# Negative maxima sent to the score rows in two parts, and one matmul fill for q, k and v with the rotary halves crossed by VectorE

## The chip, the cores and the metric

The kernel runs on one core of one Trainium2 chip. The metric is the device time of one execution in microseconds, the median over runs. Beside it there is one profiled execution, whose trace gives the span and the start and length of the instructions. Engines are named as the profile names them: PE (TensorE matmuls; PEld its weight loads), DVE (VectorE), ACT (ScalarE), POOL (GpSimd), SP (SyncE, which issues all DMAs here).

## The reference

One pre-norm decoder layer on 16 batches of 100 tokens by 128 features, in float32: causal self-attention with a rotary embedding, cross-attention with 16 heads of 64 over 1444 context rows of 96 features, and a ternary linear layer on quantized activations. Each adds to its input.

```python
def _apply_rope(t, cos, sin):
    te = t[..., 0::2]
    to = t[..., 1::2]
    oe = te * cos + to * sin
    oo = -te * sin + to * cos
...
x = x + _L0_attn_ref(_layernorm(x), wq, wk, wv)            # softmax(rope(q) rope(k)^T / sqrt(128)) v
x = x + _L0_xattn_ref(_layernorm(x), ctx_768, Wq, Wk, Wv, Wo, bo)
x = x + _L0_ffn_ref(_layernorm(x), ternary_weight, bias, act_scale)
```

## The kernel before

**Batches and steps.** Work goes batch by batch (16), a batch b in `STEPS` = 24 steps. In the cross-attention the 16 x 100 queries form Q = 1600 columns, cut in `NB` = 4 blocks of 400 (`BLK`); the 1444 keys, padded, form 12 chunks of 128. A step takes two chunks against one block, so a block is 6 steps (`BSTEPS`). In each step PE does three groups of scores (L1086: high times high, and two cross terms with the low parts) and three groups of values for the step two earlier (L1116). ACT takes the exponential twice (L615, L617), DVE makes the low part of the probabilities (`pr_lo`, L887, or L881 and L883 in a block's first step, where L881 works on partitions 64 to 99).

**Fills.** Everything else that PE does is a "fill": a small matmul into one of three PSUM banks, put between the six groups of a step by the hand-written table `AT`, and emptied ("consumed") by DVE in the same order. A fill may start when the fill three before it has been consumed (`misc_free`). A tuple in `AT` is (what, number, how many batches ahead). `MAXES` says how many of the 39 "max" fills stand in each step: they compute the scores of batch b+1 in high precision only, 13 query tiles of 128 by 3 pieces of 482 keys, and DVE reduces each (L666) to a row maximum, which the softmax needs.

**Negative maxima.** After the 39th piece DVE reduces `maxes` to `negmax` [128, 13]; the fill "negmax" in step 21 transposes it (L954); DVE copies it to `negmaxT` [13, 128] (L687); and SP sends it with two DMAs (L398, L400) into the last partition of `q_hi` of batch b+1, where the first score matmul adds it through a row of ones. PE waits for it (`row_in_s`) at the first score of a batch. Batch 0 is different: its first 7 tiles (`FIRST`, which cover 896 of 1600 queries, the first two blocks) get their maxima before the batch starts ("negmax_a"), the other 6 inside its first 9 steps ("max_b", "negmax_b").

**Self-attention.** It runs two batches ahead, one fill per stage: T1 (transposed input), QK, V, S, PT, AO, T2, in steps 3, 4, 5, 6, 8, 12 and 15. The host stacks five weights: q, q with its halves swapped, k, k with its halves swapped, v. QK makes four matmuls (L960) so that DVE can multiply q and k by cosines (L694) and the swapped ones by sines (L696) and add them (L701), all on 128 partitions. V is one matmul (L963), copied by L703.

**Loop.** Batch 0 is written out, batches 1 to 12 are a loop of 6 rounds of two batches on every engine, batches 13 to 15 are written out. The loop jumps back five times: at the starts of batches 3, 5, 7, 9 and 11. `START` lists what runs before batch 0: T1, QK, V and S of batches 0 and 1 in turn, with the four products M = Wq Wk^T by head (L1011) between them, then the first q blocks (L931) and the first maxima (L1049).

Of the kernel before, what the change touches and what calls it, by code (L numbers as in the profile page):

```python
# [35 lines left out]
def decoder_layer(nc, x_in, ctx_in, ctx_last_in, ctxT_in, wself_in, wqT_in, wkT_in, wvT_in, wo_in, bo_in,  # L36
# [4 lines left out]
    B, S, D = x_in.shape  # L41
# [34 lines left out]
    with ExitStack() as stack:  # L76
# [19 lines left out]
        wself = sb("wself", [D, 5, D])  # L96
# [28 lines left out]
        negmaxT = sb("negmaxT", [QT, P], F32R)  # L125
# [91 lines left out]
        SELF = ("T1", "QK", "V", "S", "PT", "AO", "T2")  # L217
        START = [("T1", 0), ("T1", 1), ("QK", 0), ("V", 0), ("QK", 1), ("V", 1), ("S", 0), ("S", 1),
# [5 lines left out]
        INPUT = {"QK": ("T1",), "V": ("T1",), "AO": ("PT",), "q": ("T2",), "F": ("T3",)}  # L224
# [7 lines left out]
        for what, s in zip(SELF[:-1], (3, 4, 5, 6, 8, 12)):  # L232
            AT[s].append((what, 0, 2))
# [6 lines left out]
        AT[MAX_END].append(("negmax", 0, 1))  # L240
# [15 lines left out]
        BATCH_0 = ("max_b", "negmax_b")  # L256
        for k in range(FIRST * PIECES, QT * PIECES):
            AT[(k - FIRST * PIECES) // 2].append(("max_b", k, 0))
# [40 lines left out]
        def use_of(b, wanted):  # L299

            return next(use for step in body_uses(b) for what, _, _, use, _ in step if what == wanted)
# [59 lines left out]
        def _(sp):  # L361
# [31 lines left out]
            def move_negmax(n, par, use, first=0):  # L393


                sp.wait_ge(misc_free, use + 1)
                full = Q // P
                sp.dma_start(q_hi[par][DC:DC + 1, first * P:full * P].bitcast(F32),  # L398
                             negmaxT[0:full - first, :].bitcast(F32)).then_inc(row_in_s, 16)
                sp.dma_start(q_hi[par][DC:DC + 1, full * P:Q].bitcast(F32),  # L400
                             negmaxT[full - first:QT - first, P - (Q - full * P):P].bitcast(F32)).then_inc(row_in_s, 16)
# [8 lines left out]
            def store(n, par, use):  # L410
# [5 lines left out]
            sp.wait_ge(misc_free, NSTART)  # L416
            sp.dma_start(q_hi[0][DC:DC + 1, 0:FIRST * P].bitcast(F32),
                         negmaxT[0:FIRST, :].bitcast(F32)).then_inc(row_a_in_s, 16)

            def body(b, par):  # L420
                ahead = b + 2 if isinstance(b, int) else sp.snap(b + 2)
                before = b - 1 if isinstance(b, int) else sp.snap(b - 1)
                if present(b, 0, "negmax_b"):
                    move_negmax(0, 0, use_of(0, "negmax_b"), FIRST)
                if present(b, -1):
                    move_sums(b - 1, 1 - par)
                if present(b, 2):
                    split_done(b + 1)
                    load_ctx(ahead)
                if present(b, -1):  # L430
                    store(before, 1 - par, use_of(b, "F"))
                if present(b, 1):
                    move_negmax(b + 1, 1 - par, use_of(b, "negmax"))
# [201 lines left out]
        def _(dve):  # L635
            order = Order(dve, vchain, 10)
# [18 lines left out]
            def consume(n, par, what, j, use, bank):  # L655
# [8 lines left out]
                elif what == "max":  # L664
                    t, p = divmod(j, PIECES)
                    nc.vector.tensor_reduce(maxes[:, t, p:p + 1], here[:, 0:PW], AX.X,  # L666
                                            ALU.max).then_inc(misc_free, 1)
                    if j == QT * PIECES - 1:
                        dve.wait_ge(misc_free, use + 1)
                        nc.vector.tensor_reduce(negmax[:, :], maxes[:, :, :], AX.X, ALU.max,  # L670
                                                negate=True).then_inc(negmax_done, 1)
# [8 lines left out]
                elif what == "negmax_a":  # L680
                    nc.vector.tensor_copy(negmaxT[0:FIRST, :], here[0:FIRST, 0:P]).then_inc(misc_free, 1)
                elif what == "negmax_b":
                    dve.wait_ge(row_a_in_s, 16)
                    nc.vector.tensor_copy(negmaxT[0:QT - FIRST, :], here[0:QT - FIRST, 0:P]).then_inc(misc_free, 1)
                elif what == "negmax":
                    at_least(dve, row_in_s, n * 32)
                    nc.vector.tensor_copy(negmaxT[:, :], here[0:QT, 0:P]).then_inc(misc_free, 1)  # L687
# [118 lines left out]
            for what, n in START[2:8]:  # L806
                start(what, n)
# [3 lines left out]
            for what, n in START[8:10]:  # L811
                start(what, n)
# [106 lines left out]
        def _(pe):  # L919
            def fill(n, par, what, j, use, bank, behind, ring=FILLS):  # L920
# [25 lines left out]
                elif what == "negmax_a":  # L946
                    pe.wait_ge(negmax_a_done, 1)
                    mm = nc.tensor.transpose(here[0:FIRST, 0:P], negmax[:, 0:FIRST], ident[:, :])
                elif what == "negmax_b":
                    pe.wait_ge(negmax_done, 1)  # L950
                    mm = nc.tensor.transpose(here[0:QT - FIRST, 0:P], negmax[:, FIRST:QT], ident[:, :])
                elif what == "negmax":
                    pe.wait_ge(negmax_done, n + 1)
                    mm = nc.tensor.transpose(here[0:QT, 0:P], negmax[:, :], ident[:, :])  # L954
# [3 lines left out]
                elif what == "QK":  # L958
                    for m in range(4):
                        mm = nc.tensor.matmul(here[:, m * S:(m + 1) * S], wself[:, m, :], xnT[par][:, :],  # L960
                                              start=True, stop=True)
# [67 lines left out]
            for what, n in START[2:6]:  # L1029
# [34 lines left out]
            def scores(b, par, s, i):  # L1064
# [135 lines left out]
```

## Time and profile before

| what | value |
|---|---|
| median of 3 runs | 1172.28 us (1171.85 to 1172.44) |
| the profiled execution's own time | 1173.88 us |
| its span | 1170.9 us |
| PE busy | 1136.2 us, 97% |
| DVE busy | 934.5 us, 80% |
| ACT busy | 695.5 us, 59% |
| POOL busy | 232.1 us, 20% |
| DMA | 24.40 MB, mean 21 GB/s |

The first row is what a change is measured by; the second and third belong to the execution that was traced. A busy share is an average over the span. What the time hangs on is told by the chain of work that ended last, and by what PE waited for.

### The profile page before, as it was taken

The numbers are of one execution on the slowest core, as the hardware profiler recorded it, in microseconds if no ns is written. First come the engines' busy times: TensorE is split into PE (matmuls) and PEld (weight loads), VectorE is DVE, ScalarE is ACT, GpSimd is POOL, SyncE is SP. The second block draws the span as 40 slices with busy tenths as digits, with TensorE's granted clock in tenths as the row PEclk, the third lists the DMA queues.
The fourth block names the chain that finished last, engine by engine and source line by source line (L and its number), as shares of the span: only waits on it lengthen the run. The fifth ranks groups of instructions, "written<-read, shape, count | busy, mean of one in ns | idle before, by whom it ended". The sixth has DMA issues, their size and how long they took to land.

```text
span 1170.9 us, 20390 instructions
## 1 busy us (share of the span) xinstructions
PE 1136.2 (97%) x6561; PEld 1047.5 (89%) x6561; DVE 934.5 (80%) x1691; ACT 695.5 (59%) x1001; POOL 232.1 (20%) x228
## 2 busy tenths in 40 slices
PE   6799999999999999999999999999999999999996
PEld 5588999998999899998999989999899999999995
DVE  3698888887888788787978878898788888878645
ACT  1155656656575665756657565665656566575653
POOL 3120130312203022130302213030221303112010
PEclk9799999999999999999999999999999999999998
DMA  7101010010101001010010101001010100100000
GB/s 151 41 1 42 2 41 4 1 42 5 41 3 41 4 2 40 4 41 5 9 36 1 41 5 41 3 2 42 3 41 3 41 3 2 42 2 1 3 1 4
DMA packets 12727, 24.40 MB, mean 21 GB/s; under 512 B 4934, under 2 KB 8654, under 8 KB 12494
## 3 DMA queue, kind: packets, MB, share of 16 engines
q1 hardware_dynamic: 12622, 23.00, 7.4%
q8 instruction: 65, 1.06, 0.4%
q14 instruction: 40, 0.33, 0.1%
HBM read 21.88 MB, written 0.82 MB: 19 GB/s over the span
## 4 chain that ended last, share of the span: by engine, by line
PE 91%; DVE 5%; issue 3%; ACT 1%; DMA 1%; POOL 0%; DVEq 0%; SPq 0%; POOLq 0%; ACTq 0%
PE banks L1086 35%; PE banks L1116 31%; PE banks L940 10%; PE banks L978 4%; PE banks L931 4%; PE banks L960 1%; DVE pr_lo L887 1%; PE banks L1021 1%; DVE maxes L666 1%; PE banks L1011 1%; PE banks L1049 0%; DMA q_hi<-negmaxT 0%; DVE maxes L674 0%; DVE xn L650 0%; ACT banks L617 0%
## 5 line engine op out<-in xcount | busy, mean ns | idle before, releaser
L615 ACT ACTIVATE pr_hi<-banks 128x800 fp32r<-128x800 f32 x384 | 322.4, 840 | 393.4 <-PE banks L1086 393.4
L666 DVE TENSOR_REDUCE maxes<-banks 128x1 f32<-128x482 f32 x585 | 370.4, 653 | 57.6 <-PE banks L940 53.8
L887 DVE TENSOR_TENSOR pr_lo<-banks,pr_hi 128x800 fp32r<-128x800 f32 x320 | 315.0, 985 | 56.8 <-ACT banks L617 56.4
L617 ACT ACTIVATE banks<-banks 128x800 f32<-128x800 f32 x384 | 319.8, 833 | 0.0
L940 PE MATMUL banks<-cT_hi,q_hi 96*128 96x482 f32 x585 | 223.6, 382 | 1.4 <-DVE maxes L666 1.4
L1086 PE MATMUL banks<-q_hi,cT_hi 97*128 97x400 f32 x768 | 216.7, 363 | 8.3 <-DMA q_hi<-negmaxT 7.4
L1116 PE MATMUL banks<-pr_hi,cN_hi 128*97 128x400 f32 x768 | 214.2, 346 | 0.1
L1086 PE MATMUL banks<-q_hi,cT_lo 96*128 96x400 f32 x768 | 208.5, 352 | 0.0
L1086 PE MATMUL banks<-q_lo,cT_hi 96*128 96x400 f32 x768 | 204.4, 347 | 0.0
L1116 PE MATMUL banks<-pr_hi,cN_lo 128*96 128x400 f32 x704 | 190.6, 344 | 0.0
L1116 PE MATMUL banks<-pr_lo,cN_hi 128*97 128x400 f32 x704 | 190.6, 344 | 0.0
L1086 PEld LDWEIGHTS banks<-q_hi,cT_hi 97*128 97x128 f32 x768 | 134.0, 191 | 22.1 <-issue 9.5
L1086 PEld LDWEIGHTS banks<-q_lo,cT_hi 96*128 96x128 f32 x768 | 143.4, 190 | 0.0
L1086 PEld LDWEIGHTS banks<-q_hi,cT_lo 96*128 96x128 f32 x768 | 138.6, 189 | 3.8
L1116 PEld LDWEIGHTS banks<-pr_hi,cN_hi 128*97 128x97 f32 x768 | 124.0, 163 | 12.9 <-ACT o_sb L580 0.4
L1116 PEld LDWEIGHTS banks<-pr_hi,cN_lo 128*96 128x96 f32 x704 | 113.9, 162 | 17.1
L1116 PEld LDWEIGHTS banks<-pr_lo,cN_hi 128*97 128x97 f32 x704 | 114.2, 162 | 16.1
L482 POOL TENSOR_TENSOR ve<-mv,eps 100x1 f32<-100x1 f32 x48 | 9.2, 192 | 568.7 <-DVE mv L645 568.7
L940 PEld LDWEIGHTS banks<-cT_hi,q_hi 96*128 96x128 f32 x585 | 110.0, 188 | 9.2 <-DVE maxes L666 2.2
L513 POOL TENSOR_TENSOR o_sb<-o_sb,rball 96x1600 f32<-96x1600 f32 x15 | 54.6, 3642 | 106.1 <-issue 92.3
L931 PEld LDWEIGHTS banks<-x2T,M 128*96 128x96 f32 x512 | 56.6, 172 | 4.6 <-ACT G L585 1.0
L931 PE MATMUL banks<-x2T,M 128*96 128x100 f32 x512 | 58.0, 259 | 1.1 <-ACT G L585 0.7
(116 smaller groups left out, 887.6 us busy)
## 6 DMA issues: line engine op xcount, KB each, us to landing
cT_raw<-in_ctxT SPq DMA_DIRECT2D x16, 568.5 KB
cN_raw<-in_ctx SPq DMA_DIRECT2D x16, 528.0 KB
out<-result SPq DMA_DIRECT2D x16, 50.0 KB
X<-in_x SPq DMA_DIRECT2D x1, 700.0 KB
cN_raw<-in_ctx_last SPq DMA_DIRECT2D x16, 40.5 KB
wqT<-in_wqT SPq DMA_DIRECT2D x1, 512.0 KB, 5.4
wo<-in_wo SPq DMA_DIRECT2D x1, 512.0 KB, 13.2
wkT<-in_wkT SPq DMA_DIRECT2D x1, 384.0 KB, 7.2
```

Of the source, the lines that this page charges most:

```text
L513: nc.gpsimd.tensor_tensor(out=o_sb[par][0:DC, :], in0=o_sb[par][0:DC, :], in1=rball[:, :], op=ALU.mult).then_inc(on_done, 1)
L615: nc.scalar.activation(pr_hi[:, s % RING, :].rearrange("p (a q) -> p a q", a=2), pair, ACT.Exp, scale=float(DH) ** -0.5).then_inc(hi_done, 1)
L617: nc.scalar.activation(pair, pair, ACT.Exp, scale=float(DH) ** -0.5).then_inc(exp_done, 1)
L666: nc.vector.tensor_reduce(maxes[:, t, p:p + 1], here[:, 0:PW], AX.X, ALU.max).then_inc(misc_free, 1)
L887: nc.vector.tensor_tensor(pr_lo[:, s % RING, :].rearrange("p (a q) -> p a q", a=2), banks[:, slot:slot + 2, 0:BLK], pr_hi[:, s % RING, :]. ...
L931: mm = nc.tensor.matmul(here[0:DC, i * S:(i + 1) * S], M[:, h, :], x2T[par][:, :], start=True, stop=True)
L940: mm = nc.tensor.matmul(here[:, 0:PW], q_hi[par][0:DC, qtile(t):qtile(t) + P], cT_hi[par][0:DC, PAT[p]:PAT[p] + PW], start=True, stop=True)
L960: mm = nc.tensor.matmul(here[:, m * S:(m + 1) * S], wself[:, m, :], xnT[par][:, :], start=True, stop=True)
L978: mm = nc.tensor.matmul(here[0:S, 0:D], o_sb[par][0:DC, h * S:(h + 1) * S], G[:, h, :], start=(h == 0), stop=(h == H - 1))
L1011: mm = nc.tensor.matmul(banks[:, j, i * DC:(i + 1) * DC], wqT[:, 4 * j + i, :], wkT[:, 4 * j + i, :], start=True, stop=True)
L1086: mm = nc.tensor.matmul(banks[:, ST + 2 * (s % 2) + a, 0:BLK], k, q[:, blk * BLK:(blk + 1) * BLK], start=(i == 0), stop=(i == 2))
L1116: mm = nc.tensor.matmul(banks[0:m, OUT, 0:BLK], k, e[:, r, cols], start=(first and a == 1 and i == 0), stop=(s % BSTEPS == BSTEPS - 1 and ...
```

## The change

Two edits. First, every batch now sends its negative maxima in two parts, as batch 0 did: the part of the first 7 tiles is reduced after the 21st piece (step 11), transposed by a fill in step 12 and sent by a DMA of its own; the other 6 tiles go as before in step 21. The two parts have their own tiles `negmaxT_a` and `negmaxT_b`. PE waits for part a at a batch's first score and for part b at the first step of its third block. Second, the fills QK and V become one fill QKV in step 4, without the swapped weights: DVE multiplies by the sines in two instructions of 64 partitions, each reading one half of the partitions and writing the other, then copies V, then adds.

```diff
-        wself = sb("wself", [D, 5, D])
+        wself = sb("wself", [D, 3, D])
-        negmaxT = sb("negmaxT", [QT, P], F32R)
+        negmaxT_a = sb("negmaxT_a", [FIRST, P], F32R)
+        negmaxT_b = sb("negmaxT_b", [QT - FIRST, P], F32R)
-        for what, s in zip(SELF[:-1], (3, 4, 5, 6, 8, 12)):
+        for what, s in zip(SELF[:-1], (3, 4, 6, 8, 12)):
-        AT[MAX_END].append(("negmax", 0, 1))
+        AT[12].append(("negmax_a", 0, 1))
+        AT[MAX_END].append(("negmax_b", 0, 1))
...
+            def move_negmax_a(n, par, use):
+
+                sp.wait_ge(misc_free, use + 1)
+                sp.dma_start(q_hi[par][DC:DC + 1, 0:FIRST * P].bitcast(F32),
+                             negmaxT_a[:, :].bitcast(F32)).then_inc(row_a_in_s, 16)
...
+                    if j == FIRST * PIECES - 1:
+                        dve.wait_ge(misc_free, use + 1)
+                        nc.vector.tensor_reduce(negmax[:, 0:FIRST], maxes[:, 0:FIRST, :], AX.X, ALU.max,
+                                                negate=True).then_inc(negmax_a_done, 1)
...
-                elif what == "QK":
-
-                    v = here[:, 0:4 * S].rearrange("p (a m s) -> p a m s", a=2, m=2)
+                elif what == "QKV":
+
+                    v = here[:, 0:2 * S].rearrange("p (a s) -> p a s", a=2)
                     at_least(dve, rope_done, n)
-                    order.mark(nc.vector.tensor_tensor(rt[:, :, :], v[:, :, 0, :],
-                                                       cosT[:, :].unsqueeze(1).to_broadcast([D, 2, S]), ALU.mult))
-                    nc.vector.tensor_tensor(rt2[:, :, :], v[:, :, 1, :],
-                                            sinT[:, :].unsqueeze(1).to_broadcast([D, 2, S]),
-                                            ALU.mult).then_inc(misc_free, 1)
-                    dve.wait_ge(misc_free, use + 1)
+                    order.mark(nc.vector.tensor_tensor(rt[:, :, :], v, cosT[:, :].unsqueeze(1).to_broadcast([D, 2, S]),
+                                                       ALU.mult))
+                    for to, of in ((slice(0, D // 2), slice(D // 2, D)), (slice(D // 2, D), slice(0, D // 2))):
+                        turned = nc.vector.tensor_tensor(rt2[to, :, :], v[of, :, :],
+                                                         sinT[of, :].unsqueeze(1).to_broadcast([D // 2, 2, S]), ALU.mult)
+                    order.mark(turned)
+                    nc.vector.tensor_copy(V[par][:, :], here[0:S, 2 * S:2 * S + D]).then_inc(misc_free, 1)
                     order.wait()
                     nc.vector.tensor_tensor(qk[par][:, :, :], rt[:, :, :], rt2[:, :, :], ALU.add).then_inc(rope_done, 1)
-                elif what == "V":
-                    nc.vector.tensor_copy(V[par][:, :], here[0:S, 0:D]).then_inc(misc_free, 1)
...
-                elif what == "QK":
-                    for m in range(4):
...
-                elif what == "V":
-                    mm = nc.tensor.matmul(here[0:S, 0:D], xnT[par][:, :], wself[:, 4, :], start=True, stop=True)
+                elif what == "QKV":
+                    for m in range(2):
+                        nc.tensor.matmul(here[:, m * S:(m + 1) * S], wself[:, m, :], xnT[par][:, :], start=True, stop=True)
+                    mm = nc.tensor.matmul(here[0:S, 2 * S:2 * S + D], xnT[par][:, :], wself[:, 2, :],
+                                          start=True, stop=True)
...
-                    if isinstance(b, int) and b == 0:
-                        pe.wait_ge(row_a_in_s, 16)
-                    else:
-                        pe.wait_ge(row_in_s, (b + 1) * 32)
+                    pe.wait_ge(row_a_in_s, (b + 1) * 16)
                     pe.wait_ge(cTlo_done, b + 1)
-                if blk == 2 and s % BSTEPS == 0 and i == 0 and isinstance(b, int) and b == 0:
-                    pe.wait_ge(row_in_s, 32)
+                if blk == 2 and s % BSTEPS == 0 and i == 0:
+                    pe.wait_ge(row_in_s, (b + 1) * 32)
```

In the instruction order (operation, output<-inputs, shape, times repeated; names as in the code) this is PE in steps 4 and 5 of the loop's first batch, before:

```order
L960 MATMUL banks<-xnT,wself 128x100 x4
L1116 MATMUL banks<-pr_hi,cN_hi 97x400 x2
L1116 MATMUL banks<-pr_hi,cN_lo 96x400 x2
L1116 MATMUL banks<-pr_lo,cN_hi 97x400 x2
L212 REGISTER_ALU
L940 MATMUL banks<-cT_hi,q_hi 128x482
L212 REGISTER_ALU
L1086 MATMUL banks<-q_hi,cT_hi 128x400 x2
L1086 MATMUL banks<-q_lo,cT_hi 128x400 x2
L212 REGISTER_ALU
L963 MATMUL banks<-wself,xnT 100x128
```

And the same place of the changed kernel:

```order
L967 MATMUL banks<-xnT,wself 128x100 x2
L968 MATMUL banks<-wself,xnT 100x128
L1119 MATMUL banks<-pr_hi,cN_hi 97x400 x2
L1119 MATMUL banks<-pr_hi,cN_lo 96x400 x2
L1119 MATMUL banks<-pr_lo,cN_hi 97x400 x2
L213 REGISTER_ALU
L950 MATMUL banks<-cT_hi,q_hi 128x482
L213 REGISTER_ALU
L1089 MATMUL banks<-q_hi,cT_hi 128x400 x2
L1089 MATMUL banks<-q_lo,cT_hi 128x400 x2
```

Two of the four q and k matmuls are gone, and the V matmul has moved from step 5 to stand behind the other two. DVE at the same place, before:

```order
L694 TENSOR_TENSOR rt<-banks,cosT 128x200
L696 TENSOR_TENSOR rt<-banks,sinT 128x200
L353 REGISTER_ALU
L701 TENSOR_TENSOR qk<-rt 128x200
L657 REGISTER_ALU
L666 TENSOR_REDUCE maxes<-banks 128x1
L875 REGISTER_ALU
L887 TENSOR_TENSOR pr_lo<-banks,pr_hi 128x800
L657 REGISTER_ALU
L703 COPY V<-banks 100x128
```

And changed:

```order
L705 TENSOR_TENSOR rt<-banks,cosT 128x200
L708 TENSOR_TENSOR rt<-banks,sinT 64x200 x2
L711 COPY V<-banks 100x128
L357 REGISTER_ALU
L713 TENSOR_TENSOR qk<-rt 128x200
L666 REGISTER_ALU
L675 TENSOR_REDUCE maxes<-banks 128x1
L885 REGISTER_ALU
L897 TENSOR_TENSOR pr_lo<-banks,pr_hi 128x800
```

One multiply became two, and the copy of V now stands ahead of the addition and of step 4's `pr_lo`. PE in step 12 of the same batch, changed; before, the same rows stood there without the one that reads `negmax`, and with the max fill (there L940) behind the first value group:

```order
L977 MATMUL banks<-V,prT 100x128
L1089 MATMUL banks<-q_hi,cT_lo 128x400 x2
L213 REGISTER_ALU
L950 MATMUL banks<-cT_hi,q_hi 128x482
L1119 MATMUL banks<-pr_hi,cN_hi 97x400 x2
L1119 MATMUL banks<-pr_hi,cN_lo 96x400 x2
L213 REGISTER_ALU
L958 MATMUL banks<-ident,negmax 7x128
L1119 MATMUL banks<-pr_lo,cN_hi 97x400 x2
```

One transposing matmul has been added between the value groups. The number of fills of a batch stays what it was: V is gone, negmax_a has come.

## Rows read from the trace of the kernel before

**Rows 1.** The page's busy times: us, share of span, instructions.
```profile
PE 1136.2 (97%) x6561; PEld 1047.5 (89%) x6561; DVE 934.5 (80%) x1691; ACT 695.5 (59%) x1001; POOL 232.1 (20%) x228
```

**Rows 2.** What PE waited for between 60 and 1130 us: us, times, longest.
```profile
PE banks L1086 <- DMA q_hi<-negmaxT: 4.9, 5, 1.1
PE banks L940 <- DVE maxes L666: 1.4, 2, 1.2
```

**Rows 3.** Timeline, batch starts 2 and 3: start, us, engine, line [idle before <-releaser].
```profile
195.30 0.28 DVE L687 CAST negmaxT<-banks 13x128 fp32r<-13x128 f32 x1 [0.57 <-PE banks L954]
199.38 0.53 PE L1086 MATMUL banks<-q_hi,cT_hi 97*128 97x400 f32 x2
...
269.07 0.62 PE L1086 MATMUL banks<-q_hi,cT_hi 97*128 97x400 f32 x2 [1.05 <-DMA q_hi<-negmaxT]
271.67 1.01 DVE L773 CAST cT_hi<-cT_raw 96x758 fp32r<-96x758 f32 x2 [2.12 <-issue]
```

**Rows 4.** Chain that ended last, at batch 0's start and batch 11's: start, us, what.
```profile
56.55 0.25 issue
...
817.35 0.12 PE banks L954
818.77 3.31 DMA q_hi<-negmaxT
822.08 0.68 issue
```

**Rows 5.** The same chain in steps 4 and 5 of batch 4.
```profile
349.90 0.87 PE banks L960 x8
352.82 0.22 PE banks L963 x2
```

**Rows 6.** The same chain before batch 0.
```profile
7.82 2.01 PE banks L960 x8
10.62 2.03 PE banks L960 x8
13.07 1.95 PE banks L1011 x8
```

**Rows 7.** SP's timeline, and the page's DMA issues: KB each, us from issue to landing.
```profile
3.65 0.59 SPq L367 DMA_DIRECT2D wkT<-in_wkT  x1
...
wkT<-in_wkT SPq DMA_DIRECT2D x1, 384.0 KB, 7.2
```

**Rows 8.** Stretches: length, busy us of PE, PEld, DVE, ACT, POOL, PEclk, DMA, GB/s.
```profile
62.00:63.00 1.00, 1.00 (x4) 0.93 (x4) 0.99 (x3) 0.00 (x0) 0.24 (x2) 0.50 0.00 0
63.00:64.00 1.00, 1.00 (x6) 0.72 (x5) 0.91 (x2) 0.48 (x1) 1.00 (x2) 0.96 0.00 0
70.00:80.00 10.00, 10.00 (x66) 9.20 (x67) 9.79 (x18) 5.16 (x10) 0.00 (x0) 1.00 0.01 2
```

**Rows 9.** DVE's timeline in batch 0, steps 4 to 6.
```profile
73.19 0.37 DVE L694 TENSOR_TENSOR rt<-banks,cosT 128x200 f32<-128x200 f32 x1 [0.17 <-PE banks L960]
73.48 0.35 DVE L696 TENSOR_TENSOR rt<-banks,sinT 128x200 f32<-128x200 f32 x1
73.87 0.37 DVE L701 TENSOR_TENSOR qk<-rt 128x200 f32<-128x200 f32 x1
74.15 0.66 DVE L666 TENSOR_REDUCE maxes<-banks 128x1 f32<-128x482 f32 x1
...
82.25 1.22 DVE L674 TENSOR_REDUCE maxes<-banks 128x1 f32<-128x482 f32 x2
83.49 0.58 DVE L881 TENSOR_TENSOR pr_hi<-banks,pr_hi 36x400 fp32r<-36x400 f32 x1
84.08 0.57 DVE L883 TENSOR_TENSOR pr_lo<-banks,pr_hi 128x400 fp32r<-128x400 f32 x1
```

**Rows 10.** DVE and PE in steps 4 and 5 of batch 4.
```profile
350.81 0.37 DVE L694 TENSOR_TENSOR rt<-banks,cosT 128x200 f32<-128x200 f32 x1 [0.30 <-PE banks L960]
353.46 0.52 PE L1116 MATMUL banks<-pr_hi,cN_hi 128*97 128x400 f32 x2
```

More of the change, by code:

```diff
@@ L212, in at_least @@
                 eng.wait_ge(s, value)
-        SELF = ("T1", "QK", "V", "S", "PT", "AO", "T2")
-        START = [("T1", 0), ("T1", 1), ("QK", 0), ("V", 0), ("QK", 1), ("V", 1), ("S", 0), ("S", 1),
+        SELF = ("T1", "QKV", "S", "PT", "AO", "T2")
+        START = [("T1", 0), ("T1", 1), ("QKV", 0), ("QKV", 1), ("S", 0), ("S", 1),
                  ("PT", 0), ("PT", 1), ("AO", 0), ("T2", 0)] + [("q", j) for j in range(QB)] + [
@@ L221, in decoder_layer @@
         NSTART = len(START)
-        INPUT = {"QK": ("T1",), "V": ("T1",), "AO": ("PT",), "q": ("T2",), "F": ("T3",)}
+        INPUT = {"QKV": ("T1",), "AO": ("PT",), "q": ("T2",), "F": ("T3",)}
         GBANKS = [OUT, SIDE, MISC, MISC + 1]
@@ L256, in decoder_layer @@
         BATCH_0 = ("max_b", "negmax_b")
+        assert FIRST * P >= 2 * BLK and sum(MAXES[:12]) >= FIRST * PIECES
         for k in range(FIRST * PIECES, QT * PIECES):
@@ L297, in body_uses, with use_of @@
             return found
-        def use_of(b, wanted):
-            return next(use for step in body_uses(b) for what, _, _, use, _ in step if what == wanted)
+        def use_of(b, wanted, number=0, of=None):
+            return next(use for step in body_uses(b) for what, j, away, use, _ in step
+                        if (what, j) == (wanted, number) and of in (None, away))
         def batches(eng, body):
@@ L391, in split_done, with move_negmax_b @@
                 sp.wait_ge(last_done, n + 1)
-            def move_negmax(n, par, use, first=0):
+            def move_negmax_a(n, par, use):
+                sp.wait_ge(misc_free, use + 1)
+                sp.dma_start(q_hi[par][DC:DC + 1, 0:FIRST * P].bitcast(F32),
+                             negmaxT_a[:, :].bitcast(F32)).then_inc(row_a_in_s, 16)
+            def move_negmax_b(n, par, use):
                 sp.wait_ge(misc_free, use + 1)
                 full = Q // P
-                sp.dma_start(q_hi[par][DC:DC + 1, first * P:full * P].bitcast(F32),
-                             negmaxT[0:full - first, :].bitcast(F32)).then_inc(row_in_s, 16)
+                sp.dma_start(q_hi[par][DC:DC + 1, FIRST * P:full * P].bitcast(F32),
+                             negmaxT_b[0:full - FIRST, :].bitcast(F32)).then_inc(row_in_s, 16)
                 sp.dma_start(q_hi[par][DC:DC + 1, full * P:Q].bitcast(F32),
-                             negmaxT[full - first:QT - first, P - (Q - full * P):P].bitcast(F32)).then_inc(row_in_s, 16)
+                             negmaxT_b[full - FIRST:QT - FIRST, P - (Q - full * P):P].bitcast(F32)).then_inc(row_in_s, 16)
             def move_sums(n, par):
@@ L429, in body @@
                     load_ctx(ahead)
+                if present(b, 1):
+                    move_negmax_a(b + 1, 1 - par, use_of(b, "negmax_a"))
                 if present(b, -1):
@@ L635, in _ @@
         def _(dve):
-            order = Order(dve, vchain, 10)
+            order = Order(dve, vchain, 11)
             order.base = 0
@@ L667, in consume @@
                                             ALU.max).then_inc(misc_free, 1)
+                    if j == FIRST * PIECES - 1:
+                        dve.wait_ge(misc_free, use + 1)
+                        nc.vector.tensor_reduce(negmax[:, 0:FIRST], maxes[:, 0:FIRST, :], AX.X, ALU.max,
+                                                negate=True).then_inc(negmax_a_done, 1)
                     if j == QT * PIECES - 1:
                         dve.wait_ge(misc_free, use + 1)
-                        nc.vector.tensor_reduce(negmax[:, :], maxes[:, :, :], AX.X, ALU.max,
+                        nc.vector.tensor_reduce(negmax[:, FIRST:QT], maxes[:, FIRST:QT, :], AX.X, ALU.max,
                                                 negate=True).then_inc(negmax_done, 1)
@@ L680, in consume @@
                 elif what == "negmax_a":
-                    nc.vector.tensor_copy(negmaxT[0:FIRST, :], here[0:FIRST, 0:P]).then_inc(misc_free, 1)
+                    at_least(dve, row_a_in_s, n * 16)
+                    nc.vector.tensor_copy(negmaxT_a[:, :], here[0:FIRST, 0:P]).then_inc(misc_free, 1)
                 elif what == "negmax_b":
-                    dve.wait_ge(row_a_in_s, 16)
-                    nc.vector.tensor_copy(negmaxT[0:QT - FIRST, :], here[0:QT - FIRST, 0:P]).then_inc(misc_free, 1)
-                elif what == "negmax":
@@ L686, in consume @@
                     at_least(dve, row_in_s, n * 32)
-                    nc.vector.tensor_copy(negmaxT[:, :], here[0:QT, 0:P]).then_inc(misc_free, 1)
+                    nc.vector.tensor_copy(negmaxT_b[:, :], here[0:QT - FIRST, 0:P]).then_inc(misc_free, 1)
                 elif what == "T1":
                     nc.vector.tensor_copy(xnT[par][:, :], here[:, 0:S]).then_inc(misc_free, 1)
-                elif what == "QK":
-                    v = here[:, 0:4 * S].rearrange("p (a m s) -> p a m s", a=2, m=2)
+                elif what == "QKV":
+                    v = here[:, 0:2 * S].rearrange("p (a s) -> p a s", a=2)
@@ L805, in _ @@
             dve.wait_ge(self_in_s, 16 * 3)
-            for what, n in START[2:8]:
+            for what, n in START[2:6]:
                 start(what, n)
@@ L810, in _ @@
             high_T(0, 0, 1)
-            for what, n in START[8:10]:
+            for what, n in START[6:8]:
                 start(what, n)
@@ L946, in fill @@
                 elif what == "negmax_a":
-                    pe.wait_ge(negmax_a_done, 1)
+                    pe.wait_ge(negmax_a_done, n + 1)
                     mm = nc.tensor.transpose(here[0:FIRST, 0:P], negmax[:, 0:FIRST], ident[:, :])
                 elif what == "negmax_b":
-                    pe.wait_ge(negmax_done, 1)
+                    pe.wait_ge(negmax_done, n + 1)
                     mm = nc.tensor.transpose(here[0:QT - FIRST, 0:P], negmax[:, FIRST:QT], ident[:, :])
-                elif what == "negmax":
-                    pe.wait_ge(negmax_done, n + 1)
-                    mm = nc.tensor.transpose(here[0:QT, 0:P], negmax[:, :], ident[:, :])
                 elif what == "T1":
@@ L957, in fill @@
                     mm = nc.tensor.transpose(here[:, 0:S], xn1[par][:, :], ident[0:S, 0:S])
-                elif what == "QK":
-                    for m in range(4):
-                        mm = nc.tensor.matmul(here[:, m * S:(m + 1) * S], wself[:, m, :], xnT[par][:, :],
-                                              start=True, stop=True)
-                elif what == "V":
-                    mm = nc.tensor.matmul(here[0:S, 0:D], xnT[par][:, :], wself[:, 4, :], start=True, stop=True)
+                elif what == "QKV":
[3 more added lines that the diff above has]
+                                          start=True, stop=True)
                 elif what == "S":
@@ L1028, in _ @@
             pe.wait_ge(self_in_s, 16 * 3)
-            for what, n in START[2:6]:
+            for what, n in START[2:4]:
                 start(what, n)
@@ L1169 @@
     order = np.concatenate([np.arange(0, D, 2), np.arange(1, D, 2)])
-    swapped = np.concatenate([order[D // 2:], order[:D // 2]])
     wq, wk, wv = (np.asarray(w) for w in (L0_attn_wq, L0_attn_wk, L0_attn_wv))
-    wself = np.stack([wq[order].T, wq[swapped].T, wk[order].T, wk[swapped].T, wv.T], axis=1)
+    wself = np.stack([wq[order].T, wk[order].T, wv.T], axis=1)
     i = np.arange(D // 2, dtype=np.float32)
@@ L1187 @@
         "fbias": np.asarray(L0_ffn_bias), "ascale": np.asarray(L0_ffn_act_scale).reshape(1, 1),
-        "cos": np.concatenate([cos, cos]), "sin": np.concatenate([sin, -sin]), "last": last,
+        "cos": np.concatenate([cos, cos]), "sin": np.concatenate([-sin, sin]), "last": last,
     }
```

8 lines of the change are left out of this document (3 added, 5 removed).

## The prediction

> **What bounds the kernel now.** I read the page first. PE is busy 97% of the span, DVE 80% [rows 1], so a microsecond of PE work taken from the loop should be a microsecond of time, unless PE then waits. The waits say how often it does: from 60 to 1130 us PE waits 4.9 us in five pieces for the DMA of the negative maxima and 1.4 us in two pieces for a reduction by DVE, the next largest cause [rows 2]. So two things could be won: the 4.9 us of waiting, and PE work.
>
> The timeline shows where the five pieces are: PE stands idle 1.05 us before the first score at 269.07, the start of batch 3 [rows 3]. The other four lie at the starts of batches 5, 7, 9 and 11. These are the five places where the loop jumps back. Batch 2 starts at 199.38 with no idle time in its row, only 4.08 us after DVE began the copy of its maxima [rows 3]. The same copy and the same DMAs stand at the same place in every batch. At the jump DVE too stands idle, 2.12 us before its first instruction at 271.67, and the trace lays that on issue, on no data [rows 3]. So the label "DMA" on PE's idle time is suspect: a wait is there, but the engine would not have run without it. The chain says the same for batch 11: the DMA lands at 822.08 and PE starts 0.68 us later, where before batch 0, with no jump, it starts 0.25 us after the landing [rows 4]. The landing was not what ended the wait.
>
> **The first edit: maxima in two parts.** It takes the first score's wait for the late DMA away; part a is sent a half batch earlier. By the argument above the price of what it removes is 0, with the jump as what covers it. The other bound is 4.9 us [rows 2], if the label is right and the engine could start at once. I take 0. The rule of the Trainium skill, page "Runtime: NRT & Kernel Launch", section "Instruction fetch mechanics", is that a taken branch to code outside the small instruction buffer makes the engine wait for a fetch. By that rule the idle time stays at all five places and the sum stays as below; by the label it would be 4.9 us lower. The trace sides with the rule: the 2.12 us of DVE.
>
> What it adds: one transposing fill more in batches 0 to 14. L954 takes 0.12 us of the chain [rows 4]; its cost is in the 128 columns that pass, not in the 13 or 7 that are loaded, so each of the two parts costs that. In batches 1 to 14: 14 x 0.115 = +1.6 us. DVE gets one reduction and one copy more, about 0.3 us a batch, in steps 11 and 12. SP gets one DMA, behind the context loads, due only at the next batch, some 30 us later. The wait for part b moves to the third block, 12 steps after its DMA. All of that is hidden by PE's own work.
>
> **The second edit: QKV.** The fill QK, four matmuls in eight passes, takes 0.87 us of the chain in the loop [rows 5], 0.109 a pass. Four passes go: 0.435 us a batch. V's 0.22 [rows 5] only moves. The fills for batches 3 to 15 run in batches 1 to 13: 13 x 0.435 = -5.7 us.
>
> DVE pays. Now its instructions start 0.29, 0.39 and 0.28 us after one another: 73.19, 73.48, 73.87, 74.15 [rows 9], 0.96 in all. Afterwards there are two sine multiplies. Each still has 200 elements per partition, so I give each the 0.36 us of the full one; less is the lower bound. They also start at partition 64 or write there. What such a change does is seen at L881, on partitions 64 to 99: a reduction ends at 82.25 + 1.22 = 83.47, L881 starts at 83.49, and L883 behind it starts at 84.08, when L881 has ended (84.07), whereas L696 starts 0.08 before L694's end [rows 9]. So I count whole durations: 0.39 + 0.38 + 0.38 + 0.28 = 1.43, plus 0.1 for V's copy, which no longer overlaps its neighbour: +0.6 us a batch. The page "VectorE: DVE Perf Modes", section "Two Vector instructions with no wait between them", of the Trainium skill has it as a rule: an instruction whose start quadrant differs from the last one's in the same memory is held until all before it have finished. Without the holding the extra would be 0.3 us, so the sum would be 0.3 us lower, in batch 0 alone.
>
> Does DVE's extra hurt? In the loop it matters only if a bank is freed late. In batch 4 the QKV fill would reach DVE at 350.81 - 0.435 + 0.22 = 350.6, V's copy frees the bank 1.43 us later, at 352.0. The third fill behind it, the one that needs that bank, comes after step 5's first value group: 353.46 + 0.37 - 0.435 = 353.4 [rows 10]. So 1.4 us are to spare, and the price is 0 there. In batch 0 it is not free: with the additional max fills DVE is busy 9.79 of 10 us from 70 to 80 [rows 8]. There the 0.6 counts, less the 0.17 that DVE idled for the shorter fill [rows 9], plus a transpose: +0.5 us. The saving of PE passes in that batch is then worth nothing.
>
> **Before batch 0.** The two QK fills take 2.01 and 2.03 us here [rows 6], 0.25 a pass, more than twice the loop's. Half of each goes: 2.0 us. The second one also began 0.78 us after the first ended, of which V took 0.43; the rest, a wait for DVE to free the bank, goes as well, since the fill two before is now T1. So L1011 could start 2.4 us before 13.07. Its weights bound it: they land 7.2 us after their issue at 3.65 [rows 7], at 10.9. I take 2.2 us. The input of `wself` is 128 KB smaller, which can only help. S then waits for DVE's addition, which ends by my pitches near 12.5, before L1011's 2 us are over.
>
> How much of the 2.2 reaches the end depends on the clock. The granted clock is 0.50 (1.2 GHz) until 63 us and full (2.4 GHz) from there [rows 8], 6.2 us after the first scores at 56.8 [rows 4]. If the rise moves with the work, 2.2 us are kept. If it stays at 63, 2.2 us more of the scores run at half rate, and 1.1 is kept. If it comes sooner after the scores, or the low stretch before it is shorter, up to 4 is won. I take 2.2.
>
> **Sum.** -2.2 (start) + 0.5 (batch 0) - 5.7 (passes) + 1.6 (transposes) + 0 (waits) = -5.8 us. Against the profiled execution's 1173.88 that is 1168.1. Its time stands 1.6 us above the median of the runs, so against the median, 1172.28, I say 1166.5 us.
>
> **The rivals.**
> *The waits were real.* PE no longer waits at the five starts: 4.9 us more, 1161.6. For it: the label, and a DMA that takes 3.31 us at batch 11 [rows 4]. Against it: only the jumps have the wait, and PE lags the landing by 0.68. Chance 0.13.
> *The gain is given back in small waits.* The start keeps 1.1 instead of 2.2, and the DVE extra of 0.9 us a batch makes PE wait 0.2 in each of 14 batches for a bank: +1.1 + 2.8, 1170.4, no change. For it: PE waited twice for a reduction already, 1.4 us [rows 2]. Against: no such waits in later batches. Chance 0.12.
> *The crossed multiplies are slow.* No row shows DVE reading one half of the partitions and writing the other. If each half takes over 0.36 + 0.7 = 1.06 us, the 1.4 us of slack are gone and PE waits for the bank. To be slower by 0.2% (2.3 us, about what a measurement can tell from no change) the wait must be (5.8 + 2.3)/14 = 0.58 a batch, so 1.35 us a half. At 1.6 us a half it is 14 x 1.08 - 5.8 = +9.3, 1181.6. Against it: L881 on 36 partitions with 400 elements takes 0.58, as L883 on 128 does [rows 9], so the partitions' place has no price of that size. Chance 0.05.
> The forecast itself has 0.70; its own range is 1163.5 to 1168.7, from 4 or 1.1 us at the start and 0 to 0.6 in batch 0.
>
> **Range and chances.** The range takes in the real waits and most of the small ones: 1161.0 to 1170.2. Faster by over 0.2% (under 1169.9): 0.70 + 0.13 = 0.83. Within 0.2%: 0.12. Slower: 0.05.
>
> **What would show it.** Right: the chain has four passes fewer per batch and a transpose in step 12; PE still idles about 1 us at the starts of batches 3, 5, 7, 9 and 11, now laid on issue; the halves take 0.36 us and do not overlap; batch 0's first score comes at 54.6. Wrong: those idle times are gone; the halves take over a microsecond; PE waits for max reductions in steps 4, 5, 12 or 13 of the loop; the clock rises at another distance from the first scores.

## The result, and the profile after

The changed kernel takes 1180.56 us (median of 9 runs, 1175.48 to 1182.31) against 1172.44 before, run beside it: a ratio of 1.0058, 95% interval 1.0042 to 1.0074 (the quotient of the two medians is 1.0069, inside the interval). It is slower by 0.6%, where 0.5% faster was forecast. One of the nine runs of the kernel before took 1250.07 us, far from all others, and is not in the ratio. The profiled execution took 1181.05 us.

The page of the changed kernel, answering to [rows 1], and its chain that ended last:

```profile
span 1178.9 us, 20399 instructions
PE 1136.1 (96%) x6512; PEld 1040.1 (88%) x6512; DVE 956.6 (81%) x1737; ACT 695.3 (59%) x1001; POOL 235.1 (20%) x228
...
PE 88%; DVE 7%; issue 3%; ACT 1%; DMA 0%; POOL 0%; DVEq 0%; POOLq 0%; ACTq 0%
PE banks L1089 34%; PE banks L1119 31%; PE banks L950 10%; PE banks L984 5%; PE banks L941 4%; DVE cN_hi L788 2%; DVE maxes L675 2%; DVE pr_lo L897 1%; PE banks L1027 1%; PE banks L967 1%; DVE maxes L687 1%; PE banks L1017 0%; PE banks L1055 0%; DVE x L727 0%; DVE xn L659 0%
```

Read the last line first. `DVE cN_hi L788`, 2% of the span, is `last_chunk`: one small instruction per batch that corrects the ragged last chunk of keys. It was not in the chain's line before, and the prediction never spoke of it.

PE's waits between 60 and 1130 us, answering to [rows 2]:

```profile
PE banks L1089 <- issue: 5.7, 4, 1.5
PE banks L984 <- DVE x L727: 3.9, 12, 0.4
PE banks L950 <- DVE maxes L675: 2.0, 4, 0.9
PE banks L1089 <- DVE pr_lo L897: 1.7, 1, 1.7
PE banks L958 <- DVE negmax L679: 1.5, 1, 1.5
```

The waits for the DMA are gone from the list, and the idle times they named are not: the first and the fourth row are the same five batch starts. New are twelve waits of y (L984) for `x` (L727). y is the long fill in step 12, 32 matmuls (3.7 us) that multiply the output of the cross-attention by `G`; L727 is the instruction by which DVE consumes AO, the fill with the output of the self-attention.

These rows add up to 14.8 us, 8.5 more than the two rows before. The waiting that came new must be larger, for the span grew by 8.0 us although work was saved. PE's matmul ends are modelled, so part of a wait hides in "busy". The sure measure is the distance between starts. The table takes the start of the first score matmul of each of the 384 steps from both traces and adds up the differences in step length (changed less before, us):

| place | sum | forecast |
|---|---|---|
| start, to the first score | -2.24 | -2.2 |
| batch 0 | +0.03 | +0.5 |
| steps 4 and 5 of batches 1 to 14 | -5.64 | -5.7 |
| step 12 of batches 1 to 14 | +12.46 | +1.6 |
| step 21 of batches 1 to 14 | +1.23 | 0 |
| steps 23 and 0 to 3, around the batch starts | +2.18 | 0 |
| sum (spans: 1178.9 - 1170.9) | +8.0 | -5.8 |

The savings came to a tenth of a microsecond. Step 12 took more than all of them. It was 6.06 us in nearly every batch before and is 6.2 to 7.6 now.

Here is step 12 of batch 5 in the changed kernel's timeline:

```profile
441.01 3.65 POOL L522 TENSOR_TENSOR o_sb<-o_sb,rball 96x1600 f32<-96x1600 f32 x1 [7.35 <-PE banks L1119]
442.59 2.19 DVE L788 SCALAR_TENSOR_TENSOR cN_hi<-last_hi,last,cN_raw 108x96 fp32r<-108x96 f32 x1
443.54 0.53 PE L1089 MATMUL banks<-q_hi,cT_hi 97*128 97x400 f32 x2
444.70 1.21 DVE L675 TENSOR_REDUCE maxes<-banks 128x1 f32<-128x482 f32 x2
445.40 0.49 PE L950 MATMUL banks<-cT_hi,q_hi 96*128 96x482 f32 x1 [0.38 <-DVE maxes L675]
445.95 0.17 DVE L679 TENSOR_REDUCE negmax<-maxes 128x7 f32<-128x21 f32 x1
446.14 0.99 DVE L897 TENSOR_TENSOR pr_lo<-banks,pr_hi 128x800 fp32r<-128x800 f32 x1
446.46 0.27 PE L958 MATMUL banks<-ident,negmax 128*7 128x128 f32 x1
447.05 0.34 DVE L727 SCALAR_TENSOR_TENSOR x<-banks,rsum,X 100x128 f32<-100x128 f32 x1
447.45 3.74 PE L984 MATMUL banks<-G,o_sb 96*100 96x128 f32 x32 [0.35 <-DVE x L727]
450.94 0.61 PE L1089 MATMUL banks<-q_hi,cT_hi 97*128 97x400 f32 x2
```

And the same place of the kernel before, batch 4:

```profile
368.31 3.66 POOL L513 TENSOR_TENSOR o_sb<-o_sb,rball 96x1600 f32<-96x1600 f32 x1 [7.03 <-issue]
371.40 0.69 DVE L778 SCALAR_TENSOR_TENSOR cN_hi<-last_hi,last,cN_raw 108x96 fp32r<-108x96 f32 x1
372.35 0.53 PE L1086 MATMUL banks<-q_hi,cT_hi 97*128 97x400 f32 x2
374.05 0.34 DVE L717 SCALAR_TENSOR_TENSOR x<-banks,rsum,X 100x128 f32<-100x128 f32 x1
374.99 3.66 PE L978 MATMUL banks<-G,o_sb 96*100 96x128 f32 x32
```

Three things are to be seen. First, `last_chunk` ends when GpSimd's multiply does: 442.59 + 2.19 = 444.78 against 441.01 + 3.65 = 444.66, and before 372.09 against 371.97. It takes 0.31 us where nothing is in its way. Second, everything on DVE queues behind it: two reductions, the reduction for part a, `pr_lo`, and only then AO. Third, y starts right behind AO's consumption now, at 447.45 after 447.05 + 0.34; in all of batches 1 to 13 it starts 0.05 or 0.06 us behind it. Before, it did not care about it: in batch 1 of the kernel before, where `last_chunk` took 2.46 us, y started 0.60 us ahead of the end of AO's consumption.

Why does y care? A fill needs the bank of the fill three before it. Before, y's predecessors were max, AO, max: it needed the bank of a max that DVE had long emptied. With negmax_a between, they are negmax_a, max, AO: y needs AO's bank. The edit that was counted as one matmul of 0.12 us also moved the deadline of DVE's work on AO from behind y to ahead of it.

Two more waits came with the same fill. The max fill of step 12 stands one matmul group earlier than before, and in batches 3, 4 and 5 it waited 0.56, 0.23 and 0.38 us for its bank (L950 above). In these batches y, which starts later still, waited for AO all the same. In batches 2, 6, 7 and 8 y's is the only wait in step 12. The other one is in batch 14, which has no AO: there negmax_a waits for its own reduction, which stands behind a `last_chunk` of 2.84 us. Step 12 grew by 1.8 us in this batch, part of the 12.46:

```profile
1071.19 0.27 PE L958 MATMUL banks<-ident,negmax 128*7 128x128 f32 x1 [1.53 <-DVE negmax L679]
```

### The profile page after: what moved, and what is told of

The parts are those of the page before. It is cut to its first block, busy times and chain, and to the rows that moved or that the text cites. A ratio compares the mean times of both kernels' runs of the same rounds, so it can differ in the third digit from the quotient of the medians.

```text
span 1178.9 us, 20399 instructions
## 1 busy us (share of the span) xinstructions
PE 1136.1 (96%) x6512; PEld 1040.1 (88%) x6512; DVE 956.6 (81%) x1737; ACT 695.3 (59%) x1001; POOL 235.1 (20%) x228
## 4 chain that ended last, share of the span: by engine, by line
PE 88%; DVE 7%; issue 3%; ACT 1%; DMA 0%; POOL 0%; DVEq 0%; POOLq 0%; ACTq 0%
PE banks L1089 34%; PE banks L1119 31%; PE banks L950 10%; PE banks L984 5%; PE banks L941 4%; DVE cN_hi L788 2%; DVE maxes L675 2%; DVE pr_lo L897 1%; PE banks L1027 1%; PE banks L967 1%; DVE maxes L687 1%; PE banks L1017 0%; PE banks L1055 0%; DVE x L727 0%; DVE xn L659 0%
## 5 line engine op out<-in xcount | busy, mean ns | idle before, releaser
L950 PE MATMUL banks<-cT_hi,q_hi 96*128 96x482 f32 x585 | 224.6, 384 | 2.2 <-DVE maxes L675 2.0
L950 PEld LDWEIGHTS banks<-cT_hi,q_hi 96*128 96x128 f32 x585 | 110.0, 188 | 11.6 <-DVE maxes L675 4.7
L984 PEld LDWEIGHTS banks<-G,o_sb 96*100 96x100 f32 x480 | 53.1, 167 | 8.5 <-DVE x L727 8.4
```

The source lines that it names most:

```text
L950: mm = nc.tensor.matmul(here[:, 0:PW], q_hi[par][0:DC, qtile(t):qtile(t) + P], cT_hi[par][0:DC, PAT[p]:PAT[p] + PW], start=True, stop=True)
```

## Experiments

Kernels of one group ran on one chip beside the kernel before (medians 1173.0, 1173.4, 1172.6 and 1172.8 us). Ratios are to that, with their 95% interval.

### First group: each edit alone, and two repairs

**e1, the two parts alone.** The looped kernel wants the number of fills of a batch to be a multiple of three, so two fills of one element stand in for what QKV had freed.

```diff
         AT[12].append(("negmax_a", 0, 1))
+        AT[17].append(("nil", 0, 1))
+        AT[18].append(("nil", 1, 1))
...
+                elif what == "nil":
+                    mm = nc.tensor.matmul(here[0:1, 0:1], ident[:, 0:1], ident[:, 0:1], start=True, stop=True)
```

> The maxima in two parts on the kernel before, with QK and V as they were; two tiny fills of one element (steps 17 and 18) keep the number of fills of a batch a multiple of three. Theory (the loss needs both edits: the fill in step 12 makes the long fill y wait for the bank of AO, and DVE frees it late because its last_chunk instruction runs until GpSimd's multiply ends, a collision that the faster steps 4 and 5 lengthen by 0.4 us): step 12 grows by the transpose, 0.12, and in a few batches by up to 0.4 more; with 1.6 for transposes and 1 to 2 for the tiny fills the time is 1174.5 to 1178. Rival (the new fill and its wait for the reduction cost 0.8 a batch by themselves): step 12 grows by 0.9 in each batch, 1184 to 1188. Rival of the prediction (the waits for the DMA at the five jumps were real): the five idle times go, 4.9 less than the theory says.

Measured: 1188.86 us, 1.0128 (1.0112 to 1.0143). That is above both ranges, next to the rival's, but by another sum: step 12 cost 7.7 us over the batches (0.55 a batch, up to 1.7), and the two tiny fills 9.3 us, 0.31 each. The theory's "needs both edits" fell: the parts alone lose in step 12, in the batches where `last_chunk` ends late. The five idle times stayed (1.37 to 1.64 us), and so did not belong to the DMA. My stand-ins cost too much for the total to say more; e8 repeats this cleanly.

**e2, the crossed halves alone**, V and the maxima as before.

```diff
-                    for m in range(4):
+                    for m in range(2):
```

(with the two sine multiplies of 64 partitions, as in the change)

> The crossed halves alone: two matmuls instead of four, V and the maxima as before. Theory: steps 4 and 5 give 0.43 a batch, the start about 2.0, step 12 keeps 6.06 although last_chunk runs 0.4 longer or more, since y does not need the bank of AO: 1164 to 1166. Rival (the crossed multiplies or the longer collision cost PE time by themselves): 1172 or more, with waits of PE for DVE in steps 4 to 12.

Measured: 1165.66 us, 0.9938 (0.9925 to 0.9952). Steps 4 and 5 gave 5.8 us. `last_chunk` ran 0.8 to 2.1 us in the looped batches (median 1.33, against 1.70 in the changed kernel), and step 12 stayed at 6.06 in all but one. So neither the crossing nor the longer collision costs anything by itself.

**e3, the changed kernel with negmax_a in step 14.**

```diff
-        AT[12].append(("negmax_a", 0, 1))
+        AT[14].append(("negmax_a", 0, 1))
```

> The changed kernel with the fill negmax_a in step 14 instead of 12, so that the third fill before y is a max again and not AO. Theory: step 12 is back at 6.06 with last_chunk as long as in the changed kernel (1.4 to 2.4 us); 1165.5 to 1168. Rival (DVE is late whatever y waits for, through last_chunk or the reduction of part a): step 12 stays near 7.0, 1177 to 1181.

Measured: 1169.15 us, 0.9965 (0.9951 to 0.9978). Of step 12's 12.5 us 0.8 are left, with `last_chunk` as long as before the repair (median 1.69 us in the looped batches). Its timeline in batch 4 shows DVE late and PE not waiting:

```profile
366.40 3.64 POOL L522 TENSOR_TENSOR o_sb<-o_sb,rball 96x1600 f32<-96x1600 f32 x1 [7.52 <-issue]
368.20 1.96 DVE L788 SCALAR_TENSOR_TENSOR cN_hi<-last_hi,last,cN_raw 108x96 fp32r<-108x96 f32 x1
371.84 3.66 PE L984 MATMUL banks<-G,o_sb 96*100 96x128 f32 x32
372.44 0.34 DVE L727 SCALAR_TENSOR_TENSOR x<-banks,rsum,X 100x128 f32<-100x128 f32 x1
```

y runs from 371.84, AO is consumed at 372.44. The rival is out. What is left of step 12 lies in four batches (6.28 to 6.58 us), in which DVE was latest. This repair takes away three things together: y's dependence on AO, the early place of the max fill, and negmax_a's own wait in step 12. The traces above tell them apart; no run does. The total is 1.2 us above what was expected; step 21 (+1.2) and the steps around the jumps (+0.7) hold it (below).

**e4, the changed kernel with `last_chunk` in step 14**, negmax_a left in step 12.

```diff
-                    if s == 10 and present(b, 1):
+                    if s == 14 and present(b, 1):
                         last_chunk(b + 1, 1 - par)
```

> The changed kernel with last_chunk in step 14 instead of 10, when GpSimd's long operations are over; the fill negmax_a stays in step 12. Theory (collision): last_chunk takes 0.31 us in every batch, DVE frees AO's bank in time, step 12 is 6.2; 1165.5 to 1168. Rival (the extra fill alone makes y late, since y waits for AO's bank): step 12 stays above 6.6, 1173 to 1181.

Measured: 1170.59 us, 0.9976 (0.9965 to 0.9987). `last_chunk` took 0.31 us in every batch:

```profile
L788 DVE SCALAR_TENSOR_TENSOR cN_hi<-last_hi,last,cN_raw x16: 308/310/313, 47.5 to 1071.0; 108x96 fp32r<-108x96 f32 x16
```

and step 12 was 6.15 to 6.17 in batches 1 to 13, the old 6.06 and one transpose. So the loss in step 12 needs two things, the fill negmax_a in this step and a DVE that GpSimd has held up; taking either away repairs it. The total missed the expected 1168 by 2.6 us: step 21 holds 1.2 of it, and the start of batch 7, behind a jump, lost 1.7 us in this trace.

### Second group: the jumps

**e5, the kernel before with all batches written out.**

```diff
-            with eng.Fori(0, LOOPED // 2) as i:
-                for h in (0, 1):
-                    body(i * 2 + (1 + h), 1 - h)
-            for b in range(LOOPED + 1, B):
+            for b in range(1, B):
                 body(b, b % 2)
```

> The kernel before with all 16 batches written out, no loop; the maxima are sent late in one part as before. Theory (the idle time of about 1 us at five batch starts is the jump's, not the DMA's): PE has no idle time at any batch start though the DMA is as late as it was, and the time falls by 5 us or a little more, 1166 to 1168. Rival (PE waited for the DMA): the five waits stay, 1171 to 1173.

Measured: 1164.12 us, 0.9925 (0.9911 to 0.9938), below the expected 1166 to 1168. The DMA of the maxima is as late as it was: DVE's copy ahead of it starts 4.2 us before the batch in every batch, and 4.1 to 4.2 us before the batches without a jump in the kernel before. PE's waits of this kernel from 60 to 1130 us:

```profile
PE banks L937 <- DVE maxes L663: 1.2, 1, 1.2
PE banks L954 <- DVE maxes L663: 0.5, 1, 0.5
```

No wait for it is left. The idle microsecond at five batch starts was the jump's. The gain is larger than the five idle times, 9.3 us for 4.9: the stretches from step 23 to step 3 gave 8.0 us in all, 1.6 at each of the five, a part of it outside the labelled waits.

**e6, the crossed halves alone, written out** (e2 and e5 together).

> The crossed halves alone (as in e2) with all batches written out. If the two gains are independent, e2's 1165.7 less the 5 us of the jumps: 1159.5 to 1161.5. Rival (DVE becomes late somewhere once the jumps no longer let it catch up): 1163 or more.

Measured: 1157.36 us, 0.9867 (0.9852 to 0.9882). Below the expected range, since e5 had given more than 5.

**e7, the changed kernel with both repairs** (e3's and e4's line).

> The changed kernel with both repairs: the fill negmax_a in step 14 and last_chunk in step 14. Theory: step 12 is 6.06 in every batch; what stays against the crossed halves alone (1165.7) is the 15 transposes (1.6), a slightly longer idle time at the jumps (1 to 2) less the 1 us that the merged fill wins at the start: 1166.5 to 1168.5. Rival (the loss in step 12 had a further cause): step 12 stays above 6.2 in some batches, 1170 or more.

Measured: 1168.79 us, 0.9965 (0.9951 to 0.9979), 0.3 us above the expected range. Step 12 was 6.06 in every batch from 1 to 13. No further cause is hidden there. What is left against the halves alone is 3.1 us: in the traces 1.6 of transposes, 1.2 in step 21 and 0.7 around the jumps, less 0.8 at the start.

### Third group: the two edits crossed, with no loop

Written out, the number of fills is free, so each edit can stand alone with nothing added.

> Written-out batches (as e5, 1164.1) and the maxima in two parts alone; without a loop the number of fills needs no filling up, so QK and V stay and nothing is added. Theory: step 12 grows by 0.12 plus what last_chunk ends later than 0.1 us after step 12 began; e5's trace has such ends in batches 8 to 14, 3 us in all; with 1.8 of transposes and 1.3 in step 21: 1168 to 1172. Rival (the edit is free apart from its transposes): 1165.5 to 1167.

> Written-out batches and the merged fill QKV alone, maxima in one part. Theory: as the halves alone (1157.4) with 1 us more at the start, step 12 at 6.06: 1155.5 to 1157.5. Rival (the copy of V ahead of the addition, or one fill fewer, makes PE wait somewhere): 1158.5 or more.

> Written-out batches and both edits, as changed. Theory: last_chunk ends 0.5 to 1 us after step 12 begins, since the steps before it are 0.43 shorter and GpSimd's multiply is not; step 12 is 6.6 to 7.2, so 1156.5 + 3 + 8 to 11: 1166 to 1171, as much as the parts alone although 8 us of work are gone. Rival (additive, the loss belongs to the parts alone): e8's time less 8, 1160 to 1164.

| no loop | us | against e5 | step 12, batches 1 to 14, against e5 |
|---|---|---|---|
| e5, neither edit | 1164.12 | | |
| e8, maxima in two parts | 1167.96 | +3.8 | +4.6 |
| e9, merged fill QKV | 1157.21 | -6.9 | +0.6 |
| e10, both | 1166.82 | +2.7 | +11.1 |

Ratios to the kernel before: e8 0.9967 (0.9955 to 0.9979), e9 0.9869 (0.9854 to 0.9884), e10 0.9947 (0.9933 to 0.9961). e8 came 0.04 us under its range, e9 and e10 within. The edits do not add: 3.8 - 6.9 would be -3.1, and the two together are +2.7. The 5.8 us between are paid in step 12. There the parts alone lose 1.6 us of transposes and some waits in the few batches in which `last_chunk` ends late, batches 4, 8, 9 and 14 here. With QKV beside them every batch waits. The steps before 12 have become 0.43 us shorter and GpSimd's chain has not: in e5 the multiply ends 34.08 to 34.79 us after its batch's start in batches 1 to 12, when step 12 starts at 34.53 to 34.57; in e10 it ends at 34.29 to 35.12 and step 12 starts at 34.10 to 34.12. On average the multiply even ends 0.2 us later in e10 (34.65 for 34.45), as it does in e9 (34.71); why is open. From 0.1 us behind the start of step 12 on, each tenth that `last_chunk` ends later is a tenth that step 12 grows. With its end at 34.40 step 12 takes 6.38 us (batch 1), with 35.24 it takes 7.19 (batch 4).

In e10 the largest waits of PE are these:

```profile
PE banks L980 <- DVE x L723: 2.4, 9, 0.3
PE banks L954 <- DVE negmax L675: 1.8, 1, 1.8
```

The same as with the loop: y for AO, and in batch 14, which has no self-attention to run ahead and reaches step 12 1.1 us sooner, negmax_a for its reduction.

### Fourth group: what is left

**e11, e10 with negmax_a in step 14.** The edit is e3's line.

> Both edits, batches written out, and the fill negmax_a in step 14 instead of 12 (e10 with one number changed). Theory: the whole difference between e10 (1166.8) and the merged fill alone (1157.2) is step 12, apart from 15 transposes (1.7): 1158.5 to 1160. Rival (the late DVE costs PE elsewhere too): 1162 or more.

Measured: 1158.73 us, 0.9878 (0.9861 to 0.9894): 8.1 us for one number in a table. The two parts then cost 1.5 us more than the merged fill alone, about their transposes (1.6 us in steps 14 and 15 of the trace).

**e12, e9 with `last_chunk` in step 14.** The edit is e4's line.

> The merged fill alone, batches written out, and last_chunk in step 14. e9's trace lost 0.6 us in step 12 in three batches where last_chunk ended late; without the collision 1156.3 to 1157.0. Rival (the later last_chunk collides or delays step 14 or the context loads): 1157.5 or more.

Measured: 1156.44 us, 0.9859 (0.9842 to 0.9875), 1.4% faster than before: the best of all kernels here. It keeps the maxima in one part.

## Why the prediction was wrong

- **Passes, right.** -5.64 us measured in steps 4 and 5 for -5.7.
- **Before batch 0, right in kind, and near by luck.** The first score came 2.24 us earlier, for 2.2. In the other traces with both edits (e3, e4, e7, e10, e11) it came 1.9 to 2.64 us earlier, and in e1 and e8, which leave QK as it was, still 0.5 to 0.6. The chain shows the two fills at about half length and L1017 right behind, 2.58 us earlier than before; its weights landed 6.2 us after their issue here, not 7.2, and did not bound it:

```profile
7.69 1.15 PE banks L967 x4
8.83 0.43 PE banks L968 x2
9.26 0.81 PE banks L967 x4
10.07 0.43 PE banks L968 x2
10.49 1.52 PE banks L1017 x6
```

  The granted clock rose with the work, to 0.62 in the microsecond from 60 and full (2.4 GHz) from 61 on, where it was 0.50 (1.2 GHz) until 63 before [rows 8].

- **The halves, right.** Each took 0.36 us (median 364 ns) and did not overlap its neighbours, as L881 did not [rows 9]:

```profile
351.29 0.37 DVE L705 TENSOR_TENSOR rt<-banks,cosT 128x200 f32<-128x200 f32 x1
351.69 0.74 DVE L708 TENSOR_TENSOR rt<-banks,sinT 64x200 f32<-64x200 f32 x2
352.46 0.29 DVE L711 COPY V<-banks 100x128 f32<-100x128 f32 x1
352.67 0.36 DVE L713 TENSOR_TENSOR qk<-rt 128x200 f32<-128x200 f32 x1
```

  The first ends at 351.66 and the halves start at 351.69; V's copy starts at 352.46, behind their end at 352.43. The rule of the Trainium skill, page "VectorE: DVE Perf Modes", section "Two Vector instructions with no wait between them", is that an instruction is held until all before it have finished when its start quadrant differs from the last one's in the same memory. A quadrant is 32 partitions. The start quadrant differs at both halves and at the copy, and not at L713, which starts 0.08 us ahead of the copy's end: the trace agrees. The slack of QKV's bank held too: no wait in steps 4 and 5. The slower outcome did not come by the rival that was set up for it.

- **Batch 0, mis-sized.** +0.03 us for +0.5.
- **The DMA wait, right.** It was worth nothing, and e5 shows that the jump was the cause.
- **The jumps and step 21, left out.** PE's idle times at the jumps are 1.28 to 1.68 us in the changed kernel against 0.89 to 1.05. Steps 2 and 3 give most of that back, and at four of the five places the stretch around the jump grew by 0.3 us in all. The other 1.9 of the 2.2 us fell at the start of batch 3 alone. e1's trace lost 1.9 us in the same way at batch 11, e4's 1.7 at batch 7, those of e2, e3 and e7 at no place. Step 21 grew by 0.2 us in batches 1, 3, 5, 7, 9 and 11, the first half of the loop's body, in every looped kernel with both edits (e3, e4, e7 too) and in neither e1 nor e2. In e10, with no jumps, both stretches are unchanged. The forecast had 0 for both. The causes stay open; no run varied the code of the loop alone.
- **The step that failed** is the sentence behind the cost of negmax_a: "All of that is hidden by PE's own work." It priced the fill as one transpose, +1.6 us over the batches. That much is there, but the term measured 12.5 us: 10.7 in batches 1 to 13, where y waited for AO's bank, and 1.8 in batch 14. The prediction followed the ring of banks for QKV, where it found 1.4 us to spare, and did not follow it for the fill that it added. Nor did it ask when DVE is free in step 12; it called 0.3 us of DVE work hidden without a look at that place. The clue stood in the profile of before: `last_chunk` took between 0.31 and 2.46 us for the same work.
- **The forecast's own range, mis-added.** From the terms that it names, 4 or 1.1 us at the start and 0 to 0.6 in batch 0, come 1164.2 to 1167.7, not 1163.5 to 1168.7. Nothing hung on it: the measured time lies outside both.

On the collision the Trainium skill, page "SBUF — State Buffer", section "SBUF: two separate sides", has the rule that fits: a VectorE instruction with two SBUF inputs and a GpSimd instruction that reads SBUF exclude each other for their whole length. The traces agree: `last_chunk` (L788, inputs `last_hi` and `cN_raw`) takes 0.31 us alone, and in batches 1 to 14 it ends 0.12 us behind GpSimd's instruction: the multiply, and once, in batch 1 of the kernel before, the subtraction after it (L505).

Open: why GpSimd's multiply starts between 30.4 and 31.2 us of a batch in most batches of e5, and later in some (31.7 in batch 13; 32.0 in batch 8 of e8). It follows a broadcast on the same engine, and the spread of the runs of the changed kernel (1175.5 to 1182.3 us) is of the size that such shifts make; that link is argued, not shown.

## What to carry to other kernels

An instruction added to a ring of buffers costs two things: its time, and one place for all that follow it. Ask of each long instruction behind it whose buffer it now waits for, and how late that consumer is in the worst batch, not on average.

An idle time's label names the last semaphore, not the cause. Compare places that have the same wait but not the same neighbours, and let a kernel without the neighbour decide.

A saving ahead of a collision of two other engines may feed it: what is made shorter arrives earlier at what has not moved.

## What was not expected of the hardware

- A matmul fill of one element cost PE 0.31 us each, more than the transposing fill of 128 columns in the same kernel (0.11), though its two passes deliver one column. PE's rows in e1:

```profile
393.83 0.19 PE L969 MATMUL banks<-ident 128*1 128x1 f32 x2
393.95 0.63 PE L1098 MATMUL banks<-q_hi,cT_hi 97*128 97x400 f32 x2
```

- Writing out a loop over two batches, with its five jumps, gave 9.3 us of 1173. The traces put 8.0 of them around the jumps, 1.6 us each, of which PE's labelled idle time shows 1.0.
- One VectorE instruction of 0.31 us took up to 2.84 us beside a GpSimd multiply of 3.64 us (3.10 in e10).
